# Conditioned attention layer in split float32: gamma and beta rows by transfers, another order at both ends of the kernel

## The reference, cut to what matters

```python
def sln(h, w):                                   # conditioned layer norm
    mu, var = mean(h), mean((h - mu) ** 2)       # over the features
    ln = (h - mu) / sqrt(var + EPS) * ln_g + ln_b
    return (w @ Wg.T + bg)[:, None, :] * ln + (w @ Wb.T + bb)[:, None, :]
h = sln(hidden, w)
q, k, v = split(h @ Wqkv.T + bqkv)               # 16 heads of 16
att = softmax(q @ k.T) / 16
out = (att @ v) @ Wp.T + bp
h1 = out + hidden
return sln(h1, w) + h1
```

## Time and profile before

| what | us |
|---|---|
| median of three runs | 363.55 |
| lowest and highest of them | 361.94, 365.43 |
| time of the profiled execution | 363.79 |
| its span, from the first to the last record | 361.9 |
| TensorE / VectorE / ScalarE busy in the span | 339.1 / 301.7 / 249.3 |

### The profile page before, as it was taken

One profiled execution on the slowest core, in us unless ns is written; L12 is line 12 of the kernel. 1 busy time (PEld: TensorE's weight loads), 2 busy tenths in 40 slices (PEclk: granted clock), 3 DMA queues, 4 the chain that ended last, 5 costly groups with the idle time before them and its releaser, 6 DMA issues.

```text
span 361.9 us, 8937 instructions
## 1 busy us (share of the span) xinstructions
PE 339.1 (94%) x3161; PEld 291.3 (80%) x3161; DVE 301.7 (83%) x729; ACT 249.3 (69%) x487; POOL 161.8 (45%) x203
## 2 busy tenths in 40 slices
PE   8697999999999999999999999999999999998960
PEld 4566878888898988888888989888888888886640
DVE  4678977789898989889898989898998989895463
ACT  5534586868687786868686868768686866667720
POOL 5615361526454644627173545455371723243222
PEclk9869999999999999999999999999999999999985
DMA  8195345444454544555535544444554544500000
GB/s 242 64 221 154 115 120 147 122 131 119 126 146 132 132 127 131 144 149 148 149 102 156 133 130 131 129 130 132 147 147 120 147 122 111 142 19 31 31 29 29
DMA packets 45257, 44.68 MB, mean 123 GB/s; under 512 B 6015, under 2 KB 40846, under 8 KB 45214
## 3 DMA queue, kind: packets, MB, share of 16 engines
q1 hardware_dynamic: 41470, 42.02, 42.1%
q10 hardware_dynamic: 1696, 1.57, 1.8%
q0 software_dynamic: 2048, 0.53, 0.9%
HBM read 5.79 MB, written 4.19 MB: 28 GB/s over the span
## 4 chain that ended last, share of the span: by engine, by line
PE 86%; DVE 3%; ACT 3%; DMA 3%; issue 2%; POOL 0%; POOLq 0%; SPq 0%; DVEq 0%; ACTq 0%
PE m L787 25%; PE pv L787 18%; PE st L787 18%; PE sa L787 16%; PE pv L873 4%; PE pv L947 2%; DMA wqkv<-WqkvT_dram 2%; PE m L913 2%; ACT p L511 1%; DVE mx L572 1%; DMA qst<-m_l 1%; DVE qk_l L607 1%; ACT oT L461 1%; PE pv L887 1%; PE m L887 0%
## 5 line engine op out<-in xcount | busy, mean ns | idle before, releaser
L572 DVE TENSOR_REDUCE mx<-sa 128x2 f32<-128x512 f32 x256 | 172.9, 686 | 30.2 <-PE sa L787 27.8
L511 ACT ACTIVATE p<-st 128x512 f32<-128x512 f32 x256 | 150.2, 598 | 40.4 <-PE st L787 35.7
L787 PE MATMUL st<-qst,kst 128*128 128x256 f32 x512 | 108.3, 294 | 2.0 <-ACT p L511 1.0
L787 PE MATMUL sa<-kst,qst 126*128 126x256 f32 x512 | 105.5, 288 | 2.5 <-DVE mx L572 2.2
L787 PEld LDWEIGHTS st<-qst,kst 128*128 128x128 f32 x512 | 78.1, 189 | 17.2 <-issue 13.0
L787 PEld LDWEIGHTS sa<-kst,qst 126*128 126x128 f32 x512 | 79.2, 191 | 4.8 <-DVE mx L572 4.4
L322 POOL DMA_DIRECT2D qst<-m_h x32 | 18.2, 567 | 117.5 <-DVE m_l L581 117.5
L787 PE MATMUL pv<-p,v_st 128*32 128x256 f32 x1024 | 61.9, 382 | 0.3 <-ACT p L511 0.3
L787 PEld LDWEIGHTS pv<-p,v_st 128*32 128x32 f32 x1024 | 30.0, 109 | 21.8 <-ACT p L511 2.4
L363 POOL TENSOR_TENSOR rstd<-vare,minus_half 128x4 f32<-128x4 f32 (+1 forms) x19 | 17.2, 905 | 55.8 <-DVE vare L629 36.5
L787 PE MATMUL m<-hT_h,wqkv_h 128*128 128x256 f32 x128 | 38.4, 308 | 2.2 <-DVE hT_l L651 2.2
(11 more groups left out here) (104 smaller groups left out, 556.1 us busy)
## 6 DMA issues: line engine op xcount, KB each, us to landing
qst<-qk_h SPq DMA_DIRECT2D x64, 128.0 KB, 2.4
qst<-qk_l SPq DMA_DIRECT2D x64, 128.0 KB, 2.5
kst<-qk_h SPq DMA_DIRECT2D x60, 128.0 KB, 2.5
kst<-qk_l SPq DMA_DIRECT2D x60, 128.0 KB, 2.8
xa<-x_dram SPq DMA_DIRECT2D x16, 256.0 KB, 3.0
out_dram<-y SPq DMA_DIRECT2D x16, 256.0 KB, 2.2
wqkv<-WqkvT_dram SPq DMA_DIRECT2D x1, 512.0 KB, 6.5
kst<-qk_h ACTq DMA_DIRECT2D x4, 128.0 KB, 4.4
```

The lines of the kernel that those rows point to most:

```text
L511: nc.scalar.activation(p32[:, h, :], st_ps[h % 2][:], ACT.Exp).then_inc(exp_done, 1)
L572: dve.tensor_reduce(mx[:, par(a), h // HH, (h % HH) * TT:(h % HH + 1) * TT], sa_ps[h % 2][:].rearrange("p (t n) -> p t n", t=TT), AX.X, AL ...
L787: return nc.tensor.matmul(o, l, r, start=start, stop=stop)
```

## The change

1. *Gamma and beta rows.* The rows of all batches go once to a tensor in DRAM (`gb_rows`, 32 KB); for each batch SyncE's queue issues one transfer that reads its 2 KB row for all 128 partitions (256 KB) into one of two `gb` buffers. The selection matrix, its matmul in slot 3 and ScalarE's copy of it are gone, in all 16 batches.
2. *Set-up.* The projection of batch 0 starts when the high part of h is there, with the products in another order, and the q part is finished first; VectorE makes both low parts (q, k) before it normalises batch 1; the bias row comes ahead of `turn_x(1)`; its columns are made on GpSimd; the four warm-up bursts have 8, 4, 4 and 4 matmuls instead of 9 and 5 in two. Three quarters of the clearing of `qst` for batch 1 come ahead of q of batch 0, the clearing of `kst` for batch 1 after xn of batch 1. SyncE, not ScalarE, issues the second half of k of batch 0.
3. *First step.* v of batch 0 and of batch 1 are both projected in step -1, into the score banks st0 and st1, and copied from there by ScalarE; step 0 has no v. `turn_x(2)` moves from slot 10 to slot 12. The maxima of batch 0's first half are sent by ScalarE's queue.
4. *Last step and tail.* Steps 15 to 17 are written out. The scores of batch 15 use four banks (st0, st1, sa0, sa1); the copies `oT` and `aT_h` move to VectorE there; the second half of batch 15's heads is weighed in two quarters, the last one in bank m0. For batch 15 the residual is added by TensorE (identity times x, into the bank of the projection), statistics are read from there, and a second copy of the sum, with beta in it, is built in m1, so that GpSimd adds no beta after the statistics. The last output leaves in two transfers.

The diff, cut to its core:

```diff
-S_MT1, S_GB, S_AT, S_MT0, S_XT = 1, 3, 10, 9, 10
+S_MT1, S_AT, S_MT0, S_XT = 1, 10, 9, 10
-WARM = (9, 5)
+WARM = (8, 4, 4, 4)
+V_FIRST = ((4, 4, 5, 6), (8, 9, 10, 11))
+X_FIRST = 12
+    gb_dram = nc.dram_tensor("gb_rows", (B, 2 * D), F32, kind="Internal").ap()
...
-                    sp.dma_start(raw(gb_hl[B:2 * B, :]), raw(gb_l[:])).then_inc(gbl_in, 16)
+                    for t in range(2):
+                        for low in range(2):
+                            send(1, 1, t, low)
+                if first(b + 1):
+                    sp.wait_ge(gbrow_ready, 1)
+                    sp.dma_start(gb_dram, gbrow[:]).then_inc(gb_out, 16)
...
-            stack(0, 0, 0)
-            stack(0, 1, 0)
-            steps(step, last=B + 2)
+                if has(b - 1):
+                    wait(sp, y_ready, 1 * (b - 3) + 1)
+                    if first(b - 1):
+                        sp.wait_ge(gb_out, 16)
+                    sp.dma_start(gb[:, par(b - 1)], gb_dram[b - 1].rearrange("(a n) -> a n", a=1)
+                                 .broadcast_to([P, 2 * D])).then_inc(gb_in[par(b - 1)], 16)
+
+            for g in range(2):
+                for low in range(2):
+                    send(0, g, 0, low)
+            for low in range(2):
+                send(0, 1, 1, low)
+            stack(1, 0)
+            steps(step, last=B)
+            wait(sp, y_ready, B - 2)
+            sp.dma_start(gb[:, par(B - 1)], gb_dram[B - 1].rearrange("(a n) -> a n", a=1)
+                         .broadcast_to([P, 2 * D])).then_inc(gb_in[par(B - 1)], 16)
+            wait(sp, y_ready, B - 1)
+            sp.dma_start(out_t[B - 2], y[:, par(B - 2)]).then_inc(y_out[par(B - 2)], 16)
+            for t in range(TT):
+                sp.wait_ge(yt_ready, t + 1)
+                sp.dma_start(out_t[B - 1][:, t, :], y[:, par(B - 1), t, :]).then_inc(y_out[par(B - 1)], 16)
...
+                wait(pool, gb_in[par(a)], 16 * (half(a) + 1))
+                pool.tensor_tensor(h1b[:], h1[:], gb[:, par(a), D:2 * D].rearrange("p (a n) -> p a n", a=1)
...
-                    if h == 2 and has(b - 2):
-                        wait(pool, gb_done, 1 * (b - 3) + 1)
-                        pool.tensor_copy(pick_b[:], pick[:, b - 2:b - 1].broadcast_to([P, P])).then_inc(pick_b_ready, 1)
...
+                    if h in (13, 14) and b == B - 2:
+                        add_bias(b + h - 13)
...
             pool.memset(mx[:].rearrange("p a g c -> p (a g c)"), 0.0).then_inc(mx_zero, 1)
-            pool.memset(raw(gb_hl[:]), 0.0).then_inc(gb_zero, 1)
-            pool.wait_ge(ident_ready, 1)
-            pool.tensor_tensor(pick[:], ident[:, 0:B], ident[:, B:2 * B], ALU.add).then_inc(pick_ready, 1)
-            ones_k(1, 0, 6)
+            pool.wait_ge(vecs_ready, 1)
+            pool.wait_ge(consts_ready, 2)
+            for k in range(KT):
+                o = pool.tensor_scalar(bias_cols[:, k, :], ones[:, 0:P], vecs[:, 6, k:k + 1], D ** -0.5, ALU.mult, ALU.mult)
+            o.then_inc(bias_cols_ready, 1)
+            pool.memset(v_st[:, :, :, :, HD:VC].rearrange("p a t h d -> p (a t h) d"), D ** 0.5).then_inc(v_ones_ready, 1)
             rstd_x(1)
-            ones_k(1, 6, H).then_inc(kpad_ready, 1)
-            pool.memset(v_st[:, :, :, :, HD:VC].rearrange("p a t h d -> p (a t h) d"), D ** 0.5).then_inc(v_ones_ready, 1)
+            pool.wait_ge(xn_ready, 2)
+            ones_k(1, 0, H).then_inc(kpad_ready, 1)
             pool.wait_ge(wvh_ready, 1)
             pool.tensor_tensor(wqkv_l[:, :, 2 * D:3 * D], wqkv[:, :, 2 * D:3 * D], wqkv_h[:, :, 2 * D:3 * D],
                                ALU.subtract).then_inc(wvl_ready, 1)
             pool.wait_ge(wph_ready, 1)
             pool.tensor_tensor(wp_l[:], wp[:], wp_h[:], ALU.subtract).then_inc(wpl_ready, 1)
-            pool.wait_ge(pick_ready, 1)
-            steps(step, last=B + 2)
+            steps(step)
+            maxima(B - 1, 1)
+            rstd_out(B - 3)
+            add_beta(B - 3)
+            add_beta(B - 2)
+            rstd_out(B - 2)
+            wait(pool, gb_in[par(B - 1)], 16 * (half(B - 1) + 1))
+            wait(pool, xdb_ready, B)
+            pool.tensor_tensor(xn[:], xbuf(B - 1), gb[:, par(B - 1), D:2 * D].rearrange("p (a n) -> p a n", a=1)
+                               .broadcast_to([P, TT, D]), ALU.add).then_inc(xb2_ready, 1)
+            rstd_out(B - 1)
...
-                    if h == S_GB + 1 and has(b - 2):
-                        wait(act, gb_done, 1 * (b - 2) + 1)
-                        wait(act, y_ready, 1 * (b - 3) + 1)
-                        nc.scalar.activation(gb[:], pv_ps[0][:], ACT.Copy).then_inc(gb_ready, 1)
...
+                        high_max(b + 1, 0, pv_ps[1] if first(b + 1) else m1)
+                    if h == S_MT0 + 1 and first(b + 1):
+                        for r, m, ready in ((0, m_h, mh_ready), (1, m_l, ml_ready)):
+                            act.wait_ge(ready, 1)
+                            act.dma_start(raw(qst[MAX_ROW + r:MAX_ROW + 1 + r, 0, 0:HH, :])
+                                          .rearrange("a h (t n) -> a (h t) n", t=TT),
+                                          raw(m[:, 0, :])).then_inc(max_first, 16)
...
+                    if h == 7 and first(b + 1):
+                        high_v(0, st_ps[0])
+                    if h == 12 and first(b + 1):
+                        high_v(1, st_ps[1])
...
             stack_k0(0)
             high_h_direct(1)
-            stack_k0(1)
+            act.wait_ge(bias_done, 1)
+            nc.scalar.activation(bias_b[:], pv_ps[1][:, 0:D], ACT.Copy).then_inc(bias_ready, 1)
             act.wait_ge(wv_in, 16)
...
-                    between[(1, 0)] = [lambda: low_qk(1, 0, m0, qh_ready, ql_ready)]
-                    between[(5, 0)] = [lambda: low_qk(1, 1, m1, kh_ready, kl_ready)]
+                    between[(2, 0)] = [lambda: low_qk(1, 0, m0, qh_ready, ql_ready)]
+                    between[(6, 0)] = [lambda: low_qk(1, 1, m1, kh_ready, kl_ready)]
...
             low_qk(0, 0, m0, qh_ready, ql_ready)
+            low_qk(0, 1, m1, kh_ready, kl_ready)
             norm1(1, 3)
-            low_qk(0, 1, m1, kh_ready, kl_ready)
-            for k in range(KT):
-                o = dve.tensor_scalar(bias_cols[:, k, :], ones[:, 0:P], vecs[:, 6, k:k + 1], D ** -0.5, ALU.mult, ALU.mult)
-            o.then_inc(bias_cols_ready, 1)
+            for stage in range(3):
+                norm1(2, stage)
             h_direct(1)
             low_h_direct(1)
...
+            residual(B - 3, 0)
+            low_max(B - 1, 1)
+            for stage in (1, 2, 3):
+                residual(B - 3, stage)
+            last_out(B - 2, 1)
+            normalise(B - 2, 1, 0)
+            normalise(B - 2, 1, 1)
+            last_high_att(B - 2)
+            low_att(B - 2)
+            residual(B - 3, 4)
+            last_out(B - 1, 0)
+            residual(B - 3, 5)
+            normalise(B - 1, 0, 0)
+            normalise(B - 1, 0, 1)
+            for stage in range(5):
+                residual(B - 2, stage)
+            normalise_half(0)
+            normalise_half(1)
+            low_att_half(0)
+            residual(B - 2, 5)
+            low_att_half(1)
+            for t in range(TT):
+                wait(dve, projt_done, t + 1)
+                o = dve.bn_stats(stats2[:, t, :], st_ps[t][:, 0:D])
+            o.then_inc(ln2_step, 1)
+            residual(B - 1, 2)
+            residual(B - 1, 3)
+            a = B - 1
+            wait(dve, y_out[par(a)], 16 * half(a))
+            wait(dve, gb_in[par(a)], 16 * (half(a) + 1))
+            for t in range(TT):
+                o = dve.scalar_tensor_tensor(out=y[:, par(a), t, :], in0=st_ps[t][:, 0:D], scalar=mv2[:, t, 0:1],
+                                             in1=gb[:, par(a), 0:D], op0=ALU.subtract, op1=ALU.mult)
+            o.then_inc(ln2_step, 1)
+            wait(dve, ln2_step, 4 * a + 4)
+            wait(dve, rstd_ready, 1 * a + 6)
+            dve.wait_ge(projb_done, 1)
...
+                block(0, wqkv_h, hT_h)
+                block(1, wqkv_h, hT_h)
+                pe.wait_ge(hTl_ready, 1)
+                block(0, wqkv_h, hT_l)
+                pe.wait_ge(wqkl_ready, 1)
+                block(0, wqkv_l, hT_h, q_done)
+                block(1, wqkv_h, hT_l)
+                block(1, wqkv_l, hT_h, k_done)
...
+            def last_scores(h):
+
+                b, p = B - 1, par(B - 1)
+                if h % HH == 0:
+                    wait(pe, max_in[h // HH][p], max_sent(b, h // HH))
+                if h < 2:
+                    wait(pe, exp_done, 16 * b + h - 1)
+                elif h < 4:
+                    wait(pe, max_done, 16 * b + H + h - 3)
+                else:
+                    wait(pe, exp_done, 16 * b + h - 3)
+                    o = mm(last_st[h % 4][:, t * N:(t + 1) * N], kst[:, p, h, t * P:(t + 1) * P],
...
+            def last_step():
+                last_scores(0)
+                last_scores(1)
```

(69 more changed lines are left out.)

350 lines of the change are left out of this document (230 added, 120 removed).

## The result

The changed kernel takes 351.92 us, the median of 4 runs (351.05 to 353.58), beside 362.93 for the kernel before in the same comparison: ratio 0.969, interval 0.963 to 0.976. The forecast was 351.0. The profiled execution is the slowest of the four: 353.58 us, with a span of 351.8.

A forecast was written before the change was run, and what follows sets the result against it. TensorE was taken to bound the steady part, chains of waits the first 39 and last 33 us. Terms summed to 12.9 us saved from the profiled 363.79, giving 350.9; the prediction was 351.0, range 347.3 to 356.5.

The forecast's parts named there:

- gamma and beta, 12 steps: Steps 2 to 13: removing the selection matmul saves TensorE 0.23 us a step, 2.8 us in all (1.4 to 2.9).
- step 14: Step 14: ScalarE's copy of the rows, which stood between exponentials, goes; 0.5 us saved (0.2 to 0.7).
- set-up: Before the first scores: low part of k leaves earlier, TensorE's own order bounds, scores start at 23.0; 2.4 us saved (0.4 to 4.2).
- step -1 and step 0: First steps: 0.7 us saved as a low-part wait replaces the maxima's; 1.2 saved as twelve v matmuls leave step 0.
- last scores step: Step 15: four score banks make TensorE the bound, last weighing ends 13.7 us into the step; 3.4 us saved (2.0 to 3.6).
- tail: From last weighing to span end: 16.1 us becomes 13.1 or 15.3, depending on the clock; 1.9 us saved (0.8 to 3.0).
- the tail's last wait: End of the tail: y waits for TensorE's second sum, ready at 21.4 to 23.6 us of the step, behind the root.
- signs I had listed as wrong: Would disprove the forecast: 19.7 us steps waiting for `mx`, first scores waiting for `kst`, y for the root, any `gb` wait.
- the term "at nothing": Every step's added 256 KB row transfer, issued behind an earlier batch's output and read a step later, costs nothing.
- any wait for `gb`: Anywhere in the kernel: an engine waiting for the transferred gamma and beta rows would show the forecast wrong.
- hold up the stacking transfers: Rival, chance 0.04: rows delay stacking transfers 3.1 us, 0.9 paid in each of 14 steps; no change, 363.5 us.
- confined to one DMA engine: Rival, chance 0.03: the row broadcast runs on one engine, 5.4 us more in each of 14 steps; slower, about 426 us.

The follow-up runs named there:

- e1: Kernel before, with only the gamma and beta rows brought by a transfer: 360.17 us, ratio 0.990 to the kernel before.
- e2: e1 plus the change's last step and tail with four score banks, front as in the kernel before: 355.79 us, ratio 0.978.
- e0_again: The changed kernel measured and profiled once more, nothing changed: 352.45 us, ratio 0.968 to the kernel before.
- e6: Changed kernel with each gamma and beta row of batches 0 to 13 sent twice, the second into an unread tile: 352.47 us, ratio 0.968.
- e4: Changed kernel with two score banks in the last step in place of four: 353.55 us, ratio 0.971 to the kernel before.
- e3: Changed kernel with the transpose of x of batch 2 in slot 10 of step -1 instead of 12: 351.36 us, ratio 0.965.
- e8: Changed kernel with the edits of e3 and e5 together: 349.99 us, ratio 0.960 to the kernel before.
- e5: Changed kernel with the row of batch 14 sent ahead of the output of batch 13 in SyncE's queue: 350.44 us, ratio 0.963.
- e11: e8 with the maxima of batch 0's first half sent from GpSimd's queue, as before the change, not ScalarE's: 348.54 us, ratio 0.958.

## Why the prediction was right, and where it was not

| term | forecast | measured |
|---|---|---|
| gamma and beta, 12 steps | 2.8 | 2.83 over the column of 13 steps in e1, 3.2 in the changed kernel |
| step 14 | 0.5 | 0.24 |
| set-up | 2.4 | 2.1 between the two profiles, whose first eight products with cond take 1.29 us before and 1.89 after; 3.0 with 1.89 in both (e2) |
| step -1 and step 0 | 0.7 + 1.2 | 1.2 - 2.4 |
| last scores step | 3.4 | 3.2 |
| tail | 1.9 | 2.6 |
| sum | 12.9 | 10.1; 12.2 to e0_again's span |

The time came out within a microsecond, and part of that is luck: two terms with a sum of 1.9 came as -1.2, which the others made up only in part (10.1 for 12.9 between the profiles), and the median of four executions mixes kinds 2 us apart. Three terms were right for their reasons: the rows (TensorE streams, nothing else is near; the transfers are covered, as e6 shows with twice as many), the banks (e4) and the tail's last wait. Of the last step's 3.2, though, 0.5 belongs to the rows (e1) and 2.7 to the banks.

*Set-up.* The size was right by another way, and no run takes the parts of this change one by one. I had the clock low in one late stretch and said that the stacking transfers would land before TensorE needs them. In both profiles the first scores wait for `kst<-qk_l`, 0.95 and 1.02 us; that is one of the signs I had listed as wrong. The low clock stands earlier: beside the products with cond in the slow kind (1.89 us), just behind them in the quick one (0.50 from 8.6 to 12.0 in e0_again).

*Step -1 and step 0* is the step that failed. I had the wait for the low part, its place and its cause right, but its time wrong: "there 13.4 us after the first scores". It was there at 37.28, 14.0 after, since slot 12 itself came later than I listed (the scores of batch 0 started 12.3 us after the first scores, not 11.6). So the wait was 0.93, and the q matmul stood 14.1 us after the first scores as before, where 0.7 less was forecast; in e3 it stands at 13.0. I then took no account of what standing still does to the clock behind it, though the earlier trace rows show it falling: 1.3 us in 5 of 6 profiles. And the 1.2 for the twelve v matmuls never came, with or without the wait: step 0 takes 16.15 us in e3 and 16.16 in e8, which have neither wait nor low clock, for 16.22 before. Slots 6 to 9 of step 0, where the v matmuls had stood, before and in e3 (columns of the earlier trace rows):

```profile
44.46:48.49 4.03, 3.99 (x34) 3.79 (x33) 4.03 (x9) 2.81 (x6) 3.16 (x3) 1.00 0.30 74
41.02:44.60 3.58, 2.96 (x22) 2.48 (x21) 3.58 (x9) 3.11 (x6) 3.15 (x3) 1.00 0.25 61
```

VectorE is busy all the time in both. TensorE has 1.0 us less to do there, but the four slots are only 0.45 us shorter, and slots 0 and 10 are 0.4 longer. I had divided VectorE's 13.00 by the whole 16.22 of the step; the v matmuls had stood where VectorE is full. No run puts them back, so this cause is read from the rows and not tested.

*Tail.* The forecast of y's last wait was right, and that of the quarters but for 0.7 us: they were ready at 17.7 after the step's start, not 17.0, because of the row of batch 14. That is the term "at nothing" for the new transfers: right in 13 steps, wrong in the last, where the transfer is queued behind an output that waits for VectorE, and lands only at 339.25 (4.2 us after its issue, 3.8 being the median of the 16, not 3.0). The sign "any wait for `gb`" came true once, and cost 0.9 us (e5). That the size of the tail's term fits is luck in part. At full clock, as it was, y was to end 22.3 us after the step's start and ended at 23.6, near the middle between full and half clock that I had taken; e5, without the collision, has 22.6. And behind y the span went on for 3.9 us, where I had kept 4.5 from before.

*Rivals.* None was it. The rows do not hold up the stacking transfers: e6 sends each row twice and TensorE has no wait from 55 to 305. The broadcast is not confined to one DMA engine. The Trainium skill ("DMA: Bandwidth & Descriptors", rules for kernel authors) had said so of 128 partitions, and the trace agrees: 3.8 us for 256 KB. Of its rule that spreading over queues only saves issue time, the forecast made 0; e11 measures 0.5 us between two queues, most of it issue time, as the rule has it, with 0.2 in the landing of `m_l`.

What stays open: 0.35 us of the 13 steps between e1 and the changed kernel (every step takes 19.53 us in e1 and e2 and 19.50 in the changed kernel, so it isn't one place), what decides early and late, and why TensorE's clock fell behind the wait in five profiles and not in e4's.

## What to carry to other kernels

Cut every profile at a few events and compare stage by stage: stages away from the ends repeat to 0.1 us, while medians mix kinds of executions and put e11 ahead of e8 and e4 level with its rival. A wait at a place where TensorE is sparsely busy can cost twice, itself and the clock behind it (1.2 and 1.3 us here), so move its producer two slots rather than accept "a wait takes the place of a wait". When work is moved out of a step, look which engine is full in the slots that it leaves, not in the mean of the step; and follow a new transfer into the last step, where its queue's order is another.
